# Moving the cross-attention weight products to the first stage and restructuring the text attention of a decoder kernel

## The reference, cut to what matters

```python
def bitnet_linear(x, W, b):
    w_scale = jnp.maximum(jnp.mean(jnp.abs(W)), 1e-05)
    qW = jnp.sign(W) * (jnp.abs(W) > 0.5 * w_scale).astype(W.dtype)
    i_scale = jnp.maximum(jnp.max(jnp.abs(x)), 1e-08) / 127.0
    qx = jnp.clip(jnp.round(x / i_scale), -128.0, 127.0)
    return jnp.einsum('...i,oi->...o', qx, qW) * (w_scale * i_scale) + b
...
fused = bitnet_linear(text_embeddings, W_txt, b_txt)
for Wa, ba in ((W_att0, b_att0), (W_att1, b_att1)):
    kv = bitnet_linear(image_embeds, Wa, ba)
    k = jnp.concatenate([kv, kv], axis=-1)
    scores = jnp.einsum('bse,bpe->bsp', fused, k) * inv_sqrt_e
    attn = jax.nn.softmax(scores, axis=-1)
    fused = fused + 0.1 * jnp.einsum('bsp,bpe->bse', attn, k)
```

## Time and profile before

| | |
|---|---|
| time before, median of 3 runs | 1419.61 us (1412.13 to 1420.36) |
| the profiled execution: its own time | 1425.58 us |
| its span in the trace | 1423.6 us |
| PE busy | 1112.4 us, 78% of the span |
| DVE busy | 988.6 us, 69% |
| mean granted TensorE clock | 0.893 of full speed |
| moved by DMA | 98.86 MB |

### The profile page before, as it was taken

The page is one execution under the profiler, slowest core; times in us unless marked ns, Lnnn a source line. Parts: engine busy times, 40 slices in busy tenths (PEclk is TensorE's granted clock), DMA queues, the critical chain, the costliest instruction groups (busy, mean ns, idle before and its releaser), DMA issues. The chain is left out here.

```text
span 1423.6 us, 20621 instructions
## 1 busy us (share of the span) xinstructions
PE 1112.4 (78%) x6831; PEld 926.3 (65%) x6832; DVE 988.6 (69%) x1802; ACT 475.3 (33%) x1058; POOL 395.4 (28%) x541
## 2 busy tenths in 40 slices
PE   1488888667586879999822489898988999898987
PEld 0277777655165659888711268787777778687877
DVE  7699999555856102222249999999999999999610
ACT  0111111001063043232200155555555464555453
POOL 1112222100013400000040043625445353536353
PEclk9999999866778579999966789999999999999999
DMA  6035600000000836666353000000000000000000
GB/s 225 15 115 194 235 12 4 1 0 0 1 1 32 351 112 221 248 216 232 142 220 134 0 1 1 1 7 0 7 0 7 0 7 0 0 8 0 9 8 9
DMA packets 23972, 98.86 MB, mean 69 GB/s; under 512 B 3728, under 2 KB 15184, under 8 KB 17584
## 3 DMA queue, kind: packets, MB, share of 16 engines
q1 hardware_dynamic: 16080, 72.13, 13.5%
q10 hardware_dynamic: 5200, 18.85, 4.0%
q0 software_dynamic: 2640, 7.21, 1.5%
HBM read 87.96 MB, written 21.76 MB: 77 GB/s over the span
## 5 line engine op out<-in xcount | busy, mean ns | idle before, releaser
L1850 PE MATMUL bank<-n_hA_hi_reduced,ffn_h 128*128 128x256 f32 x512 | 129.2, 294 | 14.7 <-POOL n_hA_lo_reduced L1677 14.2
L1850 PE MATMUL bank<-n_hB_hi_reduced,ffn_h 128*128 128x256 f32 x512 | 125.8, 290 | 6.1 <-ACT n_hA_lo L1976 4.4
L1850 PE MATMUL bank<-n_hA_lo_reduced,ffn_h 128*128 128x256 f32 x512 | 125.5, 287 | 0.0
L1850 PE MATMUL bank<-n_hB_lo_reduced,ffn_h 128*128 128x256 f32 x512 | 120.3, 279 | 0.0
L1850 PEld LDWEIGHTS bank<-n_hA_hi_reduced,ffn_h 128*128 128x128 f32 x512 | 101.1, 197 | 18.4 <-POOL n_hA_lo_reduced L1677 17.0
L2088 DVE TENSOR_TENSOR d_prod<-d_qk,d_xT 128x512 f32<-128x512 f32 x128 | 104.5, 856 | 0.6
L1850 PEld LDWEIGHTS bank<-n_hB_hi_reduced,ffn_h 128*128 128x128 f32 x512 | 96.5, 189 | 9.4 <-ACT n_hA_lo L1976 5.8
L1850 PEld LDWEIGHTS bank<-n_hA_lo_reduced,ffn_h 128*128 128x128 f32 x512 | 101.3, 198 | 0.2
L1850 PEld LDWEIGHTS bank<-n_hB_lo_reduced,ffn_h 128*128 128x128 f32 x512 | 96.6, 189 | 1.8 <-issue 1.7
L1511 DVE TENSOR_TENSOR e_y<-bank,e_b 128x256 f32<-128x256 f32 x23 | 9.8, 424 | 124.0 <-PE bank L1441 124.0
L1486 ACT ACTIVATE e_hT<-bank,e_b 128x128 f32<-128x128 f32 x184 | 52.4, 368 | 127.2 <-PE bank L1429 127.2
(11 more groups left out here) (327 smaller groups left out, 2687.3 us busy)
## 6 DMA issues: line engine op xcount, KB each, us to landing
e_w<-in_W SPq DMA_DIRECT2D x23, 1024.0 KB
ffn_weights<-in_F ACTq DMA_DIRECT2D x2, 5632.0 KB, 20.0
e_piece<-ffn_weights SPq DMA_DIRECT2D x11, 1024.0 KB, 4.8
ffn_h<-ffn_weights SPq DMA_DIRECT2D x2, 4096.0 KB, 18.8
ffn_w<-ffn_weights SPq DMA_DIRECT2D x3, 1024.0 KB, 6.9
expert_rows<-zero ACTq DMA_DIRECT2D x1, 2944.0 KB, 11.6
e_xs<-expert_rows SPq DMA_DIRECT2D x23, 128.0 KB, 4.5
expert_out<-e_y POOLq DMA_DIRECT2D x23, 128.0 KB, 2.0
```

The costliest lines, as they stand in the source:

```text
L1850: last = nc.tensor.matmul(F[f % 2][:, 0:PAIR], weight(w[:, k, f * P:(f + 1) * P], fast), operand(src[part][1][:, k, :], fast), start=(c == ...
```

## The change

- Keys, values, folded queries and folded outputs move from the routing stage to the first stage: their PE instructions are put between the instructions of the quantisation chain, their ACT copies become the first stage's ACT work, and the loads of the context (a second copy, x_ctx), wkv, wqT and wo1 go there too: wkv and wqT on SP's queue ahead of f1, the context and wo1 on ACT's. The first attention loses its four loads.
- In the routing stage PE has only the two rank matmuls left, and SP no longer waits for the keys and values.
- The text attention takes its scores from the plain text. PE projects the text three times per block of 512 tokens: with the sum of the two halves of the ternary weights (q_txt_sum, for the scores) and with each half (for the result). The scores of the first attention need 4 matmuls instead of 8. Those of the second are the plain text times the second keys plus the first probabilities times a small product of both keys (cross01, made in the first stage), 8 matmuls of 64 columns. Both updates are added up in PSUM and added to the text once.
- The work is cut into four streams of 512 tokens, written out in one order instead of a loop of two trips; x is quantised stream by stream; ACT scales the projections and adds their bias; the result goes to xT directly, so that the copy at L785 is gone.

The core of the diff:

```diff
 stage_bits
             for n, (name, k, width, _) in enumerate(BITS):
+                if name == "f1":
+                    sp.dma_start(wkv[:, 0, :], ins["wkv"][0:P, :]).then_inc(wkv_loaded, 16)
+                    sp.dma_start(wkv[0:DC - P, 1, :], ins["wkv"][P:DC, :]).then_inc(wkv_loaded, 16)
+                    sp.dma_start(wqT[:, :, :], ins["wqT"]).then_inc(wqT_loaded, 16)
...
+            act.dma_start(x_ctx[:, 0, :], ins["ctxT"][0:P, :]).then_inc(cxx_loaded, 16)
...
+            act.dma_start(wo1[:, :, :], ins["wo1"]).then_inc(wo1_loaded, 16)
+            keys_or_values(0, KT)
+            keys_or_values(1, VT)
+            for b in range(B):
+                folded_queries(b)
+            for b in range(B):
+                folded_outputs(b)
...
             pe.wait_ge(consts_ready, 1)
             turned(0)
             summed(0)
+            keys_or_values(0, 0, 6)
             quantised(0, ("d2v",))
+            keys_or_values(0, 6, 8)
+            keys_or_values(1, 0, 2)
             turned(1)
+            keys_or_values(1, 2, 7)
             quantised(1, ("img",))
+            keys_or_values(1, 7, 8)
+            folded_queries(0, 0)
             turned(2)
+            folded_queries(0, 1)
             quantised(2, ("att0", "att1"))
+            folded_queries(1, 0)
+            folded_queries(1, 1)
+            pe.wait_ge(wo1_loaded, 16)
+            pe.wait_ge(small_loaded, 16 * 9)
+            folded_outputs(0)
             summed(1)
...
+            pe.wait_ge(mm_done, 3)
+            for b in range(B):
+                s = slice(b * SC, (b + 1) * SC)
+                last = nc.tensor.matmul(ps_b[0:SC, b * SC:(b + 1) * SC], m.kvT[:, 0, s], m.kvT[:, 1, s],
+                                        start=True, stop=True)
+            last.then_inc(products_done, 1)
+            folded_outputs(1)
...
             ternary("txt")
+            q_txt = m.q["txt"]
+            nc.vector.tensor_tensor(m.q_txt_sum[:, :, :], q_txt[:, :, 0:P], q_txt[:, :, P:2 * P], ALU.add)
+            nc.vector.tensor_tensor(m.b_txt_sum[:, :], m.bcol[:, 4:5], m.bcol[:, 5:6], ALU.add)
...
+            v.wait_ge(products_done, 1)
+            link(nc.vector.tensor_scalar(m.cross01[:, :, :].rearrange("p b s -> p (b s)"), ps_b[0:SC, 0:B * SC], 0.2, None,
+                                         ALU.mult))
 stage_mix, on PE
+            def second(u):
...
+                for t in range(TQ):
+                    to = score[u % 3][:, (TQ + t) * SC:(TQ + t + 1) * SC]
+                    nc.tensor.matmul(to, ts[u][:, t * P:(t + 1) * P], m.kvT[:, 1, u % B * SC:(u % B + 1) * SC],
+                                     start=True, stop=False)
+                    last = nc.tensor.matmul(to, pT[u][:, 0, t * P:(t + 1) * P], m.cross01[:, u % B, :],
+                                            start=False, stop=True)
...
+            for u in range(2):
+                projected(u, 0)
+                projected(u, 1)
+                scores(u)
+                projected(u, 2)
+            turned(0, 0)
...
+            turned(2, 1)
+            updates(2)
+            turned(3, 1)
+            updates(3)
 stage_route
-            sp.wait_ge(kvx_done, 2)
             sp.wait_ge(slot_ready, 1)
...
-            keys_or_values(0)
             pe.wait_ge(hot_ready, 1)
...
-            keys_or_values(1)
-            for b in range(B):
-                folded_queries(b)
-            for b in range(B):
-                folded_outputs(b)
```

454 lines of the change are left out of this document (261 added, 193 removed).

## The result

The changed kernel takes 1433.81 us in the median of 4 runs (1430.69 to 1436.63), the kernel before beside it 1418.88 (4 runs): a ratio of 1.0114, 95% interval 1.0071 to 1.0157. I had forecast 1415 with a range up to 1431, so the forecast was wrong, and on the wrong side. The two intervals do not meet. The changed kernel took nearly the same time in both, 1433.81 and 1431.71 us; it is the kernel before that differs, 1418.88 and 1426.85 us. Both ratios lie above 1, and I take no size between 0.3 and 1.1% as shown. The profiles, one against one, say 1434.9 against 1423.6 us of span, +11.3.

The account below looks back on a forecast made before the run. It took DVE to bound the first stage, a chain through PE the mixing, PE's products then transfers the routing. Routing -30, first stage +32.3, mixing -7 gave -5 against the 1419.6 median: 1415 us, range 1394 to 1431.

Parts of the forecast that it names:

- First stage, +32.3: First stage: the moved products do not fit between the quantisation chain's links, so DVE waits; +32.3 us.
- the five waits: First stage: DVE waits for PE of 9.2, 3.15, 4.7, 3.7 and 11.0 us, 31.8 in all.
- at 2.4 GHz +10: First stage, lower bound: all PE times halved at 2.4 GHz, waits of 9.5 us, +10 us.
- Routing, -30: Routing stage: slot 10.6 us earlier, then transfers decide; first expert matmul at 493 instead of 523.1 us, -30.
- Mixing, -7: Mixing stage: PE work -1.7, first wait -3.8, shorter tail -1.3 us; sum -6.8, taken as -7.
- the sign that I had named for it: Mixing stage: forecast 67 us; the prediction counts as wrong if it takes under 60 or over 75.
- Rival D: Mixing stage: PE stays at 1.2 GHz throughout, 80 us, +6 instead of -7; whole 1428 us, chance 0.14.
- The trace disagrees for this instruction stream: First stage: products stay at 1.2 GHz, as through 22.5 us of matmuls before, against the skill's rule that activity releases the throttle.
- Rival B: First stage: PE is granted 2.4 GHz, +10 us instead of +32; whole 1393 us, chance 0.14.
- The rest of the program, 0: Stages behind the changed ones: not changed, 0 us.
- mixing at 80 us (+13): Mixing stage, upper bound: 2.4 GHz never granted, 80 us against 74, +6 instead of -7.
- instructions late (+6.6): First stage: PE instructions come late under loads, +6.6 us; a rival with the whole at 1422 us, chance 0.08.

Follow-up runs that it names:

- after_again: The changed kernel, unaltered, measured once more on another chip beside the kernel before: 1431.71 us, ratio 1.0032 (1.0021 to 1.0044).
- pad_kv: The changed kernel with the second part of context and wkv zero-filled from 64 to 128 rows: 1408.51 us beside 1425.86 of the kernel before.

## Why the prediction was wrong

- **First stage, +32.3, measured +33.9 with the attention.** Right in mechanism and size; in after_again, with wkv 2.8 us earlier, it is +30.8. Key products 0.727 (forecast 0.725), the five waits 31.4 (31.8). Single waits were off by up to 2.7: the first longer, since wkv landed 5 us later than my term had it, the last shorter by 2, with the rest of DVE's list later by about 2 us for loads. pad_kv, 57.0, is +9.6, beside my bound "at 2.4 GHz +10". That is partly luck: its first 12 products took 4.38 us, half of 8.72, mostly at 1.2 GHz, because they overlapped, and not because all times were halved.
- **Routing, -30, measured -26.6.** The last indirect transfer was issued 28.8 us after the stage's begin, as forecast (28.9). What failed is the step from there to the first matmul: I let the experts begin as soon as the transfers of the stage were through, 35.3 us after the begin. The load of the first rows was issued 7.9 us after the last indirect transfer, at 36.7, and took 2.0 more.
- **Mixing, -7, measured +2.5 (77.9), and 74.9 to 75.0 in five kernels with the same instructions.** This step failed, and a stage of over 75 us was the sign that I had named for it: of the 16 us between forecast and profile it has 9.5, routing 3.4, the first stage 1.6, the rest 2.8, less 1.2 of the feed-forward. Two terms of it were wrong. I saw that second scores alternate between 128 and 64 rows and put 0.50 us for it; it was 0.62, 3.7 us over 32 matmuls if all run at 1.2 GHz. And I took the clock as half way between its levels because it had been so before; the mean was 0.57 to 0.60 instead of 0.64. With equal rows it was 0.67 to 0.78, and the stage took 68.4 to 62.4 us, about my forecast or under it. The pair with the same rise of the clock gives 9.5 us to the rows; what else the clock does there is not parted from where the stage begins. Rival D had the direction and named the second scores, with 80 us for a clock that never rises. I gave it 0.14.
- **The clock.** "The trace disagrees for this instruction stream" was true and I stopped there. The earlier trace rows had the evidence for a question that I did not ask: why did 22.5 us of unbroken key products stay at 1.2 GHz, when shorter stretches of other work did not? Its answer, in reach through the earlier trace rows (x32 in 11.62, alternating 128 and 64 rows), was worth more than the change. Rival B (1393) needed it and got 0.14, fairly for this kernel: it did not come.
- **The rest of the program, 0, measured +2.8** in one profile. Over all runs it lies between 898.9 and 905.0 with the same instructions, so this term was noise that no forecast holds. How much of the gap between the two measured ratios is of this kind, no run shows.
- **The range** ended at 1431. My own bounds allowed more: mixing at 80 us (+13) with instructions late (+6.6) is 1434.6. I had excluded that two come together, and what came was one large miss and three small ones, all on one side.

## What to carry to other kernels

Look for f32 matmuls that accumulate over pieces with different numbers of rows (192 as 128 and 64). Here cutting them equal, 96 and 96, or filling up with zeros took a matmul from 0.727 to 0.43 us at 1.2 GHz; in the first stage and in routing the clock then rose early, and it was down to 0.25. Before moving work to where an engine is idle, ask what its own duration is made of: these products cost more through their form than through their place. And where a stage's length hangs on a clock that may rise or not, give the forecast both lengths instead of the mean.
